# Passes 3 and 4 of a four-layer graph network: six products with unread results behind each group's segment sum

## The reference

```
x = _layernorm(x + _L0_gnn_ref(x, edge_index, edge_attr_128, ...))   # edge MLP, mean over edges, node MLP
x = _layernorm(x + _L1_gnn_ref(x, src, dst, ...))                    # GCN + residual + batch norm
x = _layernorm(x + _L2_gnn_ref(x, src, dst, ...))                    # mean of neighbours
x = _layernorm(x + _L3_gnn_ref(x, edge_index, edge_type_4, edge_weight, ...))
```

```
for r in range(4): m = m + mask_r * (xj @ W[r])      # xj = x[src], one matrix per edge type
m = m * edge_weight[:, None]
out = segment_sum(m, dst, N) + x @ root + bias
```

## Time and profile before

| what | value |
|---|---|
| median of 3 runs | 5876.38 us (5876.33 to 5899.41) |
| the profiled execution: its own time | 5906.3 us |
| its span, first to last instruction | 5904.5 us |
| mean granted TensorE clock | 0.679 of full |
| TensorE matmul busy | 3182.1 us (54%) |
| VectorE busy | 1854.4 us (31%) |
| scalar engine busy | 855.8 us (14%) |
| POOL busy | 3035.0 us (51%) |
| TensorE, passes 3 and 4 (last 17 of 40 slices) | 3 to 4 tenths busy, clock 5 tenths |
| DMA, passes 3 and 4 | 1 to 2 tenths busy, 39 to 57 GB/s |

### The profile page before, as it was taken

The page is one execution under the profiler, slowest core; times in us unless marked ns, Lnnn a source line. Parts: engine busy times, 40 slices in busy tenths (PEclk is TensorE's granted clock), DMA queues, the critical chain, the costliest instruction groups (busy, mean ns, idle before and its releaser), DMA issues.

```text
span 5904.5 us, 71232 instructions
## 1 busy us (share of the span) xinstructions
PE 3182.1 (54%) x18507; PEld 2508.8 (42%) x18508; DVE 1854.4 (31%) x6372; ACT 855.8 (14%) x1655; POOL 3035.0 (51%) x3156
## 2 busy tenths in 40 slices
PE   4877778778866676456655433333433233333333
PEld 4666666667644444333433233333333222222222
DVE  4555555555631111422122122222222122222222
ACT  1333333333320000221112100000000000000000
POOL 5555555555234443333433366666665565665655
PEclk7888888888978877677877655555555555555555
DMA  5544455454434444333433122111111111111111
GB/s 173 155 153 152 147 155 153 152 154 145 139 92 126 123 112 111 96 102 102 134 101 102 52 57 56 54 52 53 53 55 51 46 46 43 44 46 44 45 42 39
DMA packets 413039, 554.49 MB, mean 94 GB/s; under 512 B 67105, under 2 KB 288033, under 8 KB 412609
## 3 DMA queue, kind: packets, MB, share of 16 engines
q0 software_dynamic: 114112, 262.48, 16.5%
q1 hardware_dynamic: 277248, 264.23, 14.8%
q10 hardware_dynamic: 21506, 26.10, 1.3%
HBM read 450.01 MB, written 102.55 MB: 94 GB/s over the span
## 4 chain that ended last, share of the span: by engine, by line
issue 22%; PE 20%; another core or an unknown queue 18%; DVEq 6%; DVE 5%; ACT 1%; POOL 0%; DMA 0%; ACTq 0%; POOLq 0%; SPq 0%
PE bank L973 9%; PE bank L951 6%; DVEq L587 2%; PE bank L961 1%; PE bank L1517 1%; DVE work L614 1%; DVEq L614 1%; DVE acc L895 1%; DVEq L845 1%; PE bank L1515 1%; DVEq L895 0%; POOL work L525 0%; DVEq L844 0%; PE bank L1352 0%
## 5 line engine op out<-in xcount | busy, mean ns | idle before, releaser
L525 POOL DMA_INDIRECT work<-table_rel,reli x1664 | 1577.9, 948 | 1076.5 <-issue 597.0
L951 PE MATMUL bank<-work 128*128 128x64 f32 x3328 | 750.6, 422 | 1088.1 <-issue 451.2
L951 PEld LDWEIGHTS bank<-work 128*128 128x128 f32 x3328 | 720.2, 329 | 1154.0 <-issue 710.1
L525 POOL DMA_INDIRECT work<-table_pre,srci x832 | 830.2, 998 | 650.3 <-PE bank L714 285.3
L624 DVE TENSOR_TENSOR acc<-acc,bank 128x64 f32 (+1 forms) x624 | 165.6, 265 | 1825.9 <-remote 1433.4
L525 POOL DMA_INDIRECT work<-table_mean,srci x312 | 296.8, 951 | 587.0 <-PE bank L961 359.9
L614 DVE TENSOR_SCALAR work<-iota,local,ew 128x64 f32<-128x64 f32 x1664 | 414.0, 325 | 478.7 <-issue 474.8
L695 PE MATMUL bank<-w1a,work 128*128 128x256 f32 x1664 | 496.7, 428 | 22.2 <-DMA work<-ea_cols 14.3
L973 PE MATMUL bank<-work,acc 128*128 128x360 f16 x2574 | 462.6, 328 | 77.5 <-issue 59.2
L729 PE MATMUL bank<-X,work 128*128 128x234 bf16 (+3 forms) x2080 | 318.8, 284 | 323.4 <-ACT X L774 192.8
L525 POOL DMA_INDIRECT work<-table_gcn,srci x312 | 295.7, 948 | 366.2 <-PE bank L961 229.0
(11 more groups left out here) (258 smaller groups left out, 2861.5 us busy)
## 6 DMA issues: line engine op xcount, KB each, us to landing
work<-adj SPq DMA_DIRECT2D x104, 720.0 KB
adj<-X SPq DMA_DIRECT2D x130, 450.0 KB
work<-ea_cols SPq DMA_DIRECT2D x208, 256.0 KB
work<-adj SPq DMA_DIRECT2D x52, 810.0 KB
work<-table_rel,reli POOLq DMA_INDIRECT x1664
work<-table_pre,srci POOLq DMA_INDIRECT x832
table_rel<-work ACTq DMA_DIRECT2D x25, 512.0 KB, 2.8
table_rel<-work SPq DMA_DIRECT2D x25, 512.0 KB
```

The lines of the kernel that those rows point to most:

```text
L525: pool.indirect_dma_start(into[:, u, :], None, tables[p], bass.IndirectOffsetOnAxis(ap=idx_of(p)[:, t:t + 1].bitcast(U32), axis=0)).then_i ...
L951: mm = pe.matmul(bank[4 + q % 2][:, 0:WIN], gat[slot][:, u, :], hot[:, q % HOTS, u * WIN:(u + 1) * WIN], start=(u == 0), stop=(u == U - 1))
```

## The change

In passes 3 and 4, TensorE issues six more products behind each group's four. They multiply the constant ones_b by four copies of the constant iota_b (128 by 512, bf16) into PSUM bank 7. Nobody reads the results, and no semaphore is added. They stand behind the matmul that raises seg_done, and ahead of the waits for the next group.

```diff
 SPLITS = 3
+KEEP = 6
...
                     mm.then_inc(seg_done[p], 1)
+                    if p >= 3:
+                        for _ in range(KEEP):
+                            pe.matmul(bank[7][:, :].rearrange("p (t f) -> p t f", f=P), ones_b[:, :],
+                                      iota_b[:, :].unsqueeze(1).broadcast_to([P, 4, P]), start=True, stop=True)
```

## The result

The changed kernel took **5985.05 us** (median of four runs, 5962.97 to 6004.97), the kernel before 5885.93 us beside it (four runs, 5876.33 to 5899.41). The ratio is **1.0166**, 95% interval 1.0114 to 1.0217: 1.7% slower, clear of no change, where faster was forecast. The profiled execution took 6000.66 us, 94.3 us of span more than that of before. Lines stand one further down as far as L957 and five further behind it (L951 is L952, L624 is L625, L614 is L615, L587 is L588, L1633 is L1638); L957 is the new product.

A forecast was written before the change was run, and what follows sets the result against it. Passes 3 and 4 were taken as bound by POOL's 40.0 us of gathers plus 9.6 us of late signals per 49.6 us round. Saving 230 us over 50 rounds and 40 in first rounds gave 5876 - 270 = 5606, said 5605; range 5400 to 5930.

The forecast's parts named there:

- The gathers' 40.0 us and the 9.6 us beside them: Passes 3 and 4: of each 49.6 us round, POOL's 32 gathers need 40.0 us; 9.6 us are not POOL's work.
- the signal is late, not the waiter: Seventh sum of a round: VectorE and POOL wake together, 20.9 us after TensorE made it, so the signal is late.
- The products' length: Six added TensorE products behind each group's sum: 1.4 us at full clock, 2.8 us at half clock.
- The clock: TensorE in passes 3 and 4: granted clock above 0.65, full from a stretch's second or third group, partly half between later groups.
- The late signal: TensorE's signal for a finished sum: lateness falls from 20.9 us to 3.1 at full clock or 6.2 at half.
- the second rival: Lateness is POOL's doing alone, products run in idle time and nothing moves: 5876 us, give or take 15; chance 0.14.
- 30.7, plus 14.3: Round in passes 3 and 4: eighth signal at 30.7 us, 14.3 to the next first add, 45.0 in all, 4.6 less.
- full-clock case: Round with full clock from the third group: eighth signal at 23.4, plus 19.5 beside gathering POOL and 3.1 late, 46.0 us.
- The sum: Passes 3 and 4: 230 us less over 50 rounds and 40 less in the two first rounds, 270 us together.
- rounds of up to 48 us: The forecast case for passes 3 and 4: rounds of 42 to 48 us, total 5455 to 5780 us; chance 0.42.
- The third: Products push a round's second to fourth sums away from POOL's restart: rounds of 52.3 us, 6010 us in all; chance 0.24.
- The first rival: POOL becomes the whole bound in passes 3 and 4: rounds of 40 to 41 us, 5385 us in all; chance 0.20.

The follow-up runs named there:

- e10: Kernel before with three of four gathers left out in passes 3 and 4, on chip D; output not the layer's: 4427.9 us.
- e3: Changed kernel with its six products narrowed from 512 to 64 columns, against the kernel before on chip B: ratio 0.9950.
- e8: Six products only behind the last four groups of each round, against the kernel before on chip C: ratio 1.0004.
- e5: Kernel before with three of four gathers left out in passes 3 and 4, on chip C; output not the layer's: 3812.8 us.
- e12: Six products only behind the first four groups of each round, against the kernel before on chip D: ratio 1.0144.

## Why the prediction was wrong

**What it is bound by.** The gathers' 40.0 us and the 9.6 us beside them were right, and so was "the signal is late, not the waiter". (An inner round takes 49.1 us on average, 0.5 us less than was taken.) Left out was where POOL itself stands still: the 9 us are its two stops, one where late signals leave it without slots, one where the next round begins late.

**The products' length** (1.4 and 2.8 us): 1.46 and 2.77 measured. **The clock**: above 0.65 was expected, 0.70 came, with full clock from the second or third group on and half clock again behind a pause (3709.74 above: 1.94 us after 6.61 us of waiting). The rule that the prediction cited from the Trainium skill, "TensorE: Matmul & The Clock Gate", that gaps send TensorE back to the low clock, agrees with that row; it wasn't what cost.

**The late signal** (3.1 us at full clock, 6.2 at half) fell. Its size doesn't go by the clock: 9.7 us late at full clock in the round above, 0.6 us at clock 0.52 in e10, and in e3 the eighth add came 5 us earlier with the clock unchanged. The rows of 3 us had been misread. POOL had just stopped in both, as the timeline of the kernel before shows:

```profile
2818.23 0.95 POOL L525 DMA_INDIRECT work<-table_mean,srci  x1 [0.30 <-issue]
...
2821.74 0.96 POOL L525 DMA_INDIRECT work<-table_mean,srci  x1 [2.56 <-remote]
```

```profile
448.66 0.96 POOL L525 DMA_INDIRECT work<-table_pre,srci  x1 [0.30 <-issue]
...
451.94 0.95 POOL L525 DMA_INDIRECT work<-table_pre,srci  x1 [2.32 <-remote]
```

The add at 2821.30 comes 2.1 us behind POOL's stop at 2819.18, the one at 451.35 comes 1.7 us behind the stop at 449.62. Each is late until POOL has stopped, like the 20.9 us of rows 3 to 5, only that the stop came sooner. So the two rows don't show what the clock does, and rows 8 are no case against the second rival. The eighth add nevertheless came as early as forecast, 29.0 us behind the first where 30.7 was said, but for another reason: POOL now stops as early as the fourth sum, its stop lets out what was held, and the rest of the sums follow at once. That this number fitted was luck.

**The step that failed** is "30.7, plus 14.3": the stretch from the eighth add to the next first was taken from a round in which POOL stood or had just restarted. It measured 21.4 us. The prediction had the row that says so, 19.5 us beside a gathering POOL, used it in its full-clock case and dropped it in the value that it took. With 21.4 and 29.0 the round is 50.4; with the forecast's own 30.7 and 19.5 it would have been 50.2, slower than the present 49.6.

**The sum.** Forecast: 4.6 us less in each of 50 rounds and 40 us less in the first rounds. Measured: 1.3 us more in each of 48, 61 us, the two first rounds 3 us less (87.9 and 87.6 became 85.6 and 86.8), and 7 us more at the ends of the passes. The forecast's own range for rounds of up to 48 us should have ended at 5756, not 5780. The remaining 29 us of the spans' difference is ahead of pass 3 in unchanged code; four runs on chip D began pass 3 at 3258, 3263, 3271 and 3280 us, 22 us apart, so part of it at least is scatter.

**The rivals.** The third was nearest: the products push the second to fourth sums away from POOL's restart, 52.3 us a round and 6010 us. It had place and sign right. Its condition was wrong: it was to decide by an eighth signal later than 35.3 us at half clock, and the eighth came earlier, at a higher clock. The first rival (POOL the whole bound, rounds of 40 to 41 us) is what chip C shows in e8, whose time is that of the kernel before there (1.0004), so it owes nothing to the products. The second (lateness is POOL's doing alone) had the cause right as far as e10 shows it, and there "nothing moves" was wrong, since POOL's doing has a time in the round that the products shift.

## What to carry to other kernels

When a wait goes, ask where in the other engines' schedule the work behind it lands. A stretch whose length was read while a neighbour stood still must be read again beside the busy neighbour; here that single figure was the sign. Before lateness is put down to an engine's clock, look at what every other engine did at the moment when it ended, and for rows that hold one cause and vary the other; and where an effect of this size rides on it, measure on more than one chip.

## What the runs showed of the hardware

- Chips differ. On one of the chips used, the kernel before took 4764 us, on the others 5808 to 5928. On that chip no signal was late in passes 3 and 4 of e5 to e8, and POOL went through each of the two passes without a stop in e8; its gathers took 0.947 us there and 0.948 in the earlier trace rows.
- On the others, the signals that TensorE raises soon after POOL's restart are mostly prompt, and the later ones come behind POOL's next stop (2.3 us in the round above, 3.5 in the earlier trace rows) or after many us within the gathers. In the 48 inner rounds of the kernel before, 155 of the 384 adds come more than 5 us late, 70 of them in a stop of POOL (3.5 us behind its begin in the median, 4.7 at most) and 85 while it gathers. VectorE's register steps stretch from 0.18 or 0.02 to 0.70 us in stretches of POOL's gathers (e12), not in e10. TensorE's matmuls keep their length (1.00 us for the fourth sum).
- The Trainium skill, "SBUF — State Buffer", section "SBUF: two separate sides", says that on the engines' side only VectorE and GpSimd share a port and that TensorE waits on no one there. The matmuls' unchanged length agrees. What is late is TensorE's signal, of which the sentence says nothing; no run here shows by which path the gathers hold it, or whether it is POOL's work or its DMA traffic.
